# The first expert of a mixture kernel in another order, and every fourth input tile kept on chip

## The reference, cut to what matters

```python
# x: (32, 128, 1024): 4096 tokens of 1024 values
y   = einsum('bct,bcd->bdt', x, w0[cond])            # one 128x128 matrix per batch entry
probs = softmax(y @ gate_w.T)                        # 64 experts
w, sel = top_k(probs, 8);  w = w / sum(w)
# each expert takes its first CAP = 256 tokens, in token order
h   = silu(inp @ wg[e]) * (inp @ wu[e])              # 256 x 384
out = h @ wd[e]                                      # 256 x 1024
x   = x + sum over the experts of w * out, at the token's row
x   = x + second layer (one adapter matrix per batch entry, then a base product
          with a two-of-eight gated low-rank part)
```

## Time and profile before

| | |
|---|---|
| median of three runs | 2400.86 us (2400.47 to 2400.88) |
| the profiled execution | 2414.42 us, span 2412.7 us |
| mean granted clock of PE | 0.994 of full speed |
| PE busy | 2371.8 us (98% of the span) |
| DVE, ACT, POOL busy | 1739.5, 1374.4, 1408.7 us |
| DMA | 582.35 MB, mean 241 GB/s |

### The profile page before, as it was taken

One profiled execution on the slowest core, in us unless ns is written; L12 is line 12 of the kernel. 1 busy time (PEld: TensorE's weight loads), 2 busy tenths in 40 slices (PEclk: granted clock), 3 DMA queues, 4 the chain that ended last, 5 costly groups with the idle time before them and its releaser, 6 DMA issues.

```text
span 2412.7 us, 35618 instructions
## 1 busy us (share of the span) xinstructions
PE 2371.8 (98%) x12877; PEld 2089.1 (87%) x12877; DVE 1739.5 (72%) x2905; ACT 1374.4 (57%) x2288; POOL 1408.7 (58%) x1032
## 2 busy tenths in 40 slices
PE   6998999999999999999999999999999999999999
PEld 4677888888888888888888888888879999999999
DVE  4877888888888887888888888887862255555554
ACT  4766777777677776777777777777751111111110
POOL 4107887777777777777777777777710032222221
PEclk9999999999999999999999999999999999999999
DMA  8988998989999899998989989899875254444441
GB/s 295 366 293 286 292 282 282 279 276 292 286 289 282 277 285 284 280 285 274 283 282 284 281 278 280 278 289 279 276 205 110 76 148 129 129 129 129 129 120 56
DMA packets 249457, 582.35 MB, mean 241 GB/s; under 512 B 82745, under 2 KB 106682, under 8 KB 249154
## 3 DMA queue, kind: packets, MB, share of 16 engines
q1 hardware_dynamic: 182306, 401.18, 50.8%
q0 software_dynamic: 55584, 160.02, 25.6%
q10 hardware_dynamic: 11392, 18.88, 2.1%
HBM read 460.71 MB, written 123.45 MB: 242 GB/s over the span
## 4 chain that ended last, share of the span: by engine, by line
PE 89%; ACT 1%; DVE 1%; DMA 1%; issue 1%; SPq 0%; ACTq 0%; DVEq 0%
PE ps L762 25%; PE ps L775 21%; PE ps L869 16%; PE ps L761 12%; PE ps L827 5%; PE ps L758 4%; PE ps L862 2%; PE ps L759 2%; PE ps L842 1%; PE ps L725 1%; ACT HR L1020 0%; DMA raw<-in_L_ffn_wd 0%; DMA bmR<-accd 0%; DVE LR L1435 0%; DMA x<-in_L_ffn_base_w 0%
## 5 line engine op out<-in xcount | busy, mean ns | idle before, releaser
L762 PE MATMUL ps<-XX,HR 128*128 128x512 f32 x2688 | 958.6, 396 | 0.0
L761 PE MATMUL ps<-XX,LR 128*128 128x256 f32 x2688 | 750.4, 279 | 0.0
L546 POOL DMA_INDIRECT Xg<-yd,idx x504 | 648.0, 1286 | 166.2 <-issue 152.6
L1435 DVE TENSOR_TENSOR LR<-raw,HR 128x1536 fp32r<-128x1536 f32 x384 | 657.3, 1752 | 5.7 <-issue 3.7
L762 PEld LDWEIGHTS ps<-XX,HR 128*128 128x128 f32 x2688 | 505.3, 188 | 103.7
L1020 ACT ACTIVATE HR<-raw 128x1536 fp32r<-128x1536 f32 x384 | 556.4, 1478 | 16.5 <-DMA raw<-in_L_ffn_wd 11.5
L761 PEld LDWEIGHTS ps<-XX,LR 128*128 128x128 f32 x2688 | 507.0, 189 | 17.7 <-issue 0.2
L568 POOL DMA_INDIRECT accd<-ot,toki x128 | 254.2, 1986 | 157.4 <-ACT ot L1074 136.0
L869 PE MATMUL ps<-MH,xT 128*128 128x392 f32 x1536 | 337.2, 345 | 0.0
L775 PE MATMUL ps<-HR,hH 128*128 128x512 f32 x768 | 300.0, 391 | 4.8 <-DVE hL L1479 4.8
L775 PE MATMUL ps<-LR,hH 128*128 128x512 f32 x768 | 303.6, 395 | 0.0
(11 more groups left out here) (203 smaller groups left out, 3344.0 us busy)
## 6 DMA issues: line engine op xcount, KB each, us to landing
raw<-in_L_ffn_wd SPq DMA_DIRECT2D x128, 768.0 KB
raw<-in_L_ffn_wg SPq DMA_DIRECT2D x126, 768.0 KB
raw<-in_L_ffn_wu SPq DMA_DIRECT2D x126, 768.0 KB
xt<-in_x SPq DMA_DIRECT2D x32, 512.0 KB
yd<-yrow ACTq DMA_DIRECT2D x32, 512.0 KB, 6.7
x<-accd SPq DMA_DIRECT2D x32, 512.0 KB, 5.0
out<-osb SPq DMA_DIRECT2D x31, 512.0 KB, 2.9
accd<-xt SPq DMA_DIRECT2D x24, 512.0 KB
```

What stands on the lines that cost most here:

```text
L546: eng.indirect_dma_start(Xg[:, c, q, :], None, yd4, bass.IndirectOffsetOnAxis(ap=idx4[:, e % 4, i:i + 1], axis=0))\
L761: eng.matmul(bank(out, 0, CAP), wl, xx[:, 0:CAP], start=False, stop=False)
L762: mm = eng.matmul(bank(out), wh, xx, start=False, stop=(k == 7))
L1435: eng.tensor_tensor(LR[:, (n + 2) % NHL, :], raw[:, n % NRAW, :], HR[:, (n + 2) % NHL, :].bitcast(F32), ALU.subtract).then_inc(s_L, 1)
```

## The change

Seven things are changed, all of them at the seam of stage 1 and the first expert.

1. `turn_0`: the identity products ahead of `direct_rows` (4) go, and 10 and 44 become 8 and 20.
2. The eight tiles with i % 4 = 3 are not copied from DRAM to DRAM. Seven of them are loaded to places of their own (`xkA`, `xkB`, `xkC`, found by `xin(i)`), which lie in HR and LR buffers that stage 1 doesn't use; the last one stays in `xt[:, 3]`. `store_kept(n)` stores them to `acc` from there: four behind unit 1, four behind unit 5. Semaphores `d_ak[0]` and `d_ak[1]` tell of the two groups.
3. New waits on them: ACT's split of unit 4 on group 0 and of unit 6 on group 1, DVE's split of unit 4 and `turn_x(1, 0)` on group 1, `scatter(0)` on both.
4. SP's units 0 to 3 wait for the row stores of tiles 25 to 28 in place of 28 to 31.
5. DVE: `direct_token(0)` and `direct_token(1)` stand ahead of `tiles(NB - 6)`, and the first waits for all row stores (`d_ys`).
6. ACT, first expert: `uB`, the load of the Silu table, then `high_0`, then `dA`, `dB` and the parts' chain, with shares and `store_w` between the first and the second part, and the unit splits of expert 1 behind the third part except `gA`.
7. DVE, first expert: `uA` ahead of `low_0`; `join(0)` ahead of the last `weigh`/`invert`, which are spread around `product(0)`; `dB`, the turns and sums for expert 1 between the parts; `column(0)`, `column(1)`, `index(2)` behind the third part, then the splits of expert 1.

From the second expert on the order is the same as before.

```diff
-            rest = [i for i in range(NB) if i % 4 >= NS]
-
-            def fill(n):
-                i = rest[n]
-                if n >= 2:
-                    eng.wait_ge(d_ad[n % 2], 16 * (n // 2))
-                eng.dma_start(acc[i * P:(i + 1) * P, :], x_r[i * P:(i + 1) * P, :]).then_inc(d_ad[n % 2], 16)
+            def store_kept(n):
+                i = 4 * n + NS
+                eng.wait_ge(d_x[NS], 16 * (n + 1))
+                eng.dma_start(acc[i * P:(i + 1) * P, :], xin(i)).then_inc(d_ak[n // KEEP], 16)
 
             for n in range(len(units)):
                 if n < NRAW:
-                    i = NB - NRAW + n
+                    i = NB - NRAW - 3 + n
                     eng.wait_ge(d_ys[i % NY], 16 * (i // NY + 1))
...
                 load_unit(n)
-                if n == 7:
-                    for k in range(FILL):
-                        fill(k)
-                if n >= 8 and n - 8 + FILL < len(rest):
-                    fill(n - 8 + FILL)
+                if n == 1:
+                    for k in range(KEEP):
+                        store_kept(k)
+                if n == NRAW + 1:
+                    for k in range(KEEP, NB // 4):
+                        store_kept(k)
...
             def turn_0():
                 eng.wait_ge(s_yr, NB)
-                keep_busy(4)
                 direct_rows()
-                keep_busy(10)
+                keep_busy(8)
                 eng.wait_ge(s_tok, 2)
-                keep_busy(44)
+                keep_busy(20)
...
@@ ACT
+                if n == NRAW:
+                    eng.wait_ge(d_ak[0], 16 * KEEP)
+                if n == 6:
+                    eng.wait_ge(d_ak[1], 16 * KEEP)
...
             split("uA", 0)
+            split("uB", 0)
+            eng.activation(sil[:, 0:1], pf[:, 0:1], ACT.Silu)
             for n in range(4):
                 high_0(n)
-            split("uB", 0)
+            split("dA", 0)
+            split("dB", 0)
+            copy_2(0)
+            silu(0)
+            high_h(0)
             for i in range(NB - 4, NB):
                 share(i)
             store_w(NB - 1)
-            eng.activation(sil[:, 0:1], pf[:, 0:1], ACT.Silu)
-            split("dA", 0)
+            split("gA", 1)
+            copy_2(1)
+            silu(1)
+            high_x(1, 0)
+            high_h(1)
+            high_x(1, 1)
+            copy_2(2)
+            silu(2)
+            spread(2)
+            high_h(2)
+            for k in ("uA", "gB", "uB", "dA"):
+                split(k, 1)
...
@@ DVE
             direct_slots()
-            tiles(NB - 6)
             direct_token(0)
             direct_token(1)
+            tiles(NB - 6)
...
+                if n == NRAW:
+                    eng.wait_ge(d_ak[1], 16 * KEEP)
...
             index(1)
+            split("uA", 0)
             for n in range(4):
                 low_0(n)
-            split("uA", 0)
             split("uB", 0)
             for i in range(NB - 3, NB):
                 tiles(i)
             table_rows()
-            for i in range(NB - 4, NB):
+            split("dA", 0)
+            join(0)
+            for i in range(NB - 4, NB - 2):
                 weigh(i)
                 invert(i)
-            split("dA", 0)
+            product(0)
+            for i in range(NB - 2, NB):
+                weigh(i)
+                invert(i)
+            low_h(0)
+            split("dB", 0)
+            join(1)
+            turn_x(1, 0)
+            product(1)
+            turn_x(1, 1)
+            low_h(1)
+            count(2)
+            token(2)
+            join(2)
+            low_x(1, 0)
+            product(2)
+            low_x(1, 1)
+            low_h(2)
+            column(0)
+            column(1)
+            index(2)
+            for k in ("gA", "uA", "gB", "uB"):
+                split(k, 1)
+            count(3)
+            token(3)
+            split("dA", 1)
```

76 lines of the change are left out of this document (34 added, 42 removed).

## The result

The changed kernel takes 2408.86 us (median of 8 runs, 2407.58 to 2412.56). The kernel before, run beside it, takes 2401.67 us (8 runs, 2400.47 to 2402.71). The ratio is 1.0032, with a 95% interval of 1.0024 to 1.0041: the change costs 7.2 us. The prediction was 2396.5 us with a range of 2391.0 to 2400.6, so it has the wrong sign and misses its range.

A forecast was written before the change was run, and what follows sets the result against it. PE was taken to bound the kernel, at 25.0 us an expert from the third on. PE 4.4 us earlier at the third part of up(2), taken over to the median 2400.86 us, gave 2396.5 us, range 2391.0 to 2400.6.

The forecast's parts named there:

- What bounds the kernel: Whole kernel: PE, busy 2371.8 of 2412.7 us; only its idle or low-clock time in the first experts can be won.
- The sum: PE at the third part of up(2): 254.9 - 250.5 = 4.4 us earlier, then 25.0 us an expert as before.
- Its eight issues took 11.3 us: POOL's gather_x(2): starts at 204.5 instead of 207.39, keeps its 11.3 us, last issue out at 215.8.
- The start: First expert: direct_token(0) near 165.0, 1.4 us earlier; high_0 at 175.3, 5.4 us earlier; up(0) at 178.5 instead of 183.92.
- The new wait: DVE's split of dA in expert 0 waits about 6 us for the kept stores, the last landing near 188.
- the stores are hidden: Rival on the kept stores: they land before about 184, 6.5 to 10 us won, 2392 us; chance 0.24.
- DVE's walk: DVE's queue in the first expert, walked from 188.1: index(2) done at 204.5, before at 205.27.
- From the last issue to `join(3)`: Behind gather_x(2): 3 us to land and turn, then low_x and join; from 215.8 to join(3) at 222.9.
- The clock: Third part of up(1): PE idles 4.2 us, restarts at half clock and loses 2.0 us.
- The gap at `up(0)`: PE idle 2.8 us between transposes and up(0): at most 2.0 us of low clock, covered, so nothing in the sum.
- POOL behind `gather_x(2)`: POOL's 1.62 us idle ahead of scatter(0) goes; last gather for expert 3 and join(6) come 4.5 us earlier.
- slower by over 0.2%: Rival: direct_token(0) waits for all 32 row stores, landing d after 165.0; over 0.2% slower from d = 9.2 us; chance 0.10.

The follow-up runs named there:

- experiment 15: Kernel before with fewer identity products, join(2) moved first, and gather_x(e + 2) ahead of scatter(e - 1) on POOL for every expert: 2465.51 us, ratio 1.0269.
- experiment 5: The changed kernel again, no edit, for a second profile: 2421.12 us, ratio 1.0026 to the kernel before.
- experiment 1: The kernel before again, no edit, for a second profile: 2413.83 us, ratio 0.9997.
- experiment 6: Changed kernel with count(3) and token(3) between the second and third of DVE's four splits behind index(2): 2420.38 us, ratio 1.0020 to the kernel before.
- experiment 13: Changed kernel with index(2) behind DVE's four splits instead of ahead of them: 2408.36 us, ratio 1.0028 to the kernel before.
- experiment 3: Changed kernel with the second group of four kept stores issued behind unit 3 instead of unit 5: 2419.05 us, ratio 1.0023 to the kernel before.
- experiment 7: Changed kernel with count(2), token(2), spread(2) and index(2) moved earlier: 2415.27 us, ratio 1.0001 to the kernel before.
- experiment 8: Changed kernel with 14 identity products added behind the transposes, ahead of up(0): 2420.04 us, ratio 1.0023 to the kernel before.
- experiment 9: Changed kernel with raw weight loads waiting for row stores 28 to 31, as in the kernel before: 2420.76 us, ratio 1.0029 to the kernel before.
- experiment 4: Kernel before with only the kept tiles, their stores and waits, in its own queue orders: 2414.27 us, ratio 1.0000.
- experiment 16: Kernel before with kept tiles and 28 identity products, but old queue orders, no early SP start, no row-store wait: 2402.46 us, ratio 1.0002.
- experiment 10: Kernel before with the changed kernel's turn_0 and ACT and DVE orders, but old fills, SP queue and buffers, no row-store wait: 2418.57 us, ratio 1.0010.
- experiment 2: Kernel before with only fewer identity products, none ahead of direct_rows, then 8 and 20: 2409.38 us, ratio 0.9984.

## Why the prediction was wrong

**What bounds the kernel** was read rightly: PE, and only its idle and slow stretches in the first experts. From the third part of `up(2)` to the end of the span every profile but one has 2154.7 to 2159.5 us, whatever its kernel; the one is experiment 15 (2205.2), which makes the scatter late. The place of the loss was foretold too: PE idles before the third part of `up(1)` and restarts at half clock. Its size was not.

**The sum, redone.** The prediction had PE at the third part of `up(2)` at 250.6; experiment 5, with stage 1 as long as in the profile before, has 261.63. That is 6.7 us later than before (254.93) and 7.9 later than in experiment 1 (253.76), so a loss of the measured size (6.5 us beside experiment 5, 7.2 in the first comparison) already stands at this product; what single executions differ by behind it allows no finer account. The forecast is missed by 11.0 us: 3.1 at the start of `up(0)` (181.59, predicted 178.5), 7.3 from there to the third part of `up(1)` (52.4, predicted 45.1), and 0.6 from there on (27.6, predicted 27.0).

**The largest step that failed: "Its eight issues took 11.3 us", taken over to a place where they take 16.5.** The prediction moved `gather_x(2)` to the start of DVE's four splits and kept its old length. The first issue takes 7.2 us there, 3.9 before two splits, and 0.95 behind them (experiments 5, 6, 13); only in experiment 3 it takes 2.2 before four. That is 5.2 of the 11.0 us, and 5.2 of the 5.6 us by which `join(3)` comes later behind `up(0)` in the first profile than predicted (50.0, 44.4). This step alone doesn't decide the sign. With 2.21 us for the first issue in the profile of experiment 3, or 3.88 in that of experiment 6, the kernels are no better by the ratios (1.0023 and 1.0020, beside 1.0026), and the rows are turned later behind their issue. Only the earlier index, which takes the gather out of the run's start and puts it ahead, wins 5.9 us (experiment 7), and that just makes up the loss. The steps below are needed for the rest. The Trainium skill has a mechanism near this one (SBUF — State Buffer, section "SBUF: two separate sides"): a DMA issued from GpSimd's queue has its descriptors written by GpSimd, and VectorE can lock it out of the ports they share while it runs an operation in a two-port mode. For operations with two inputs in SBUF, as the splits are, it names contention only against a GpSimd operation that reads SBUF; the issue has its indices in SBUF (`idx`), so it may be one. I had not weighed that rule. The traces show the issue waiting for a split (0.95 us without, 2.24 under one); why one issue waits for four of them no run here shows.

**The start.** `direct_token(0)` was to be 1.4 us earlier, at 165.0. In six profiles of the changed kernel and its variants (experiments 3 and 5 to 9; the kernel before has 165.66 beside them) it lies between 165.44 and 168.60, never earlier by more than 0.2 us and mostly later: what PE saved in front of it, something in the last tiles took back. The early weights (change 4) are the likeliest. Where stage 1 is long, every profile with them has `Gj` at 166.57 or later; without them it is at 165.66 or earlier but for 166.42 in the earlier trace rows and 167.41 in experiment 4, both with the old order and all identity products. Where it is short, those with them have 154.26 or later, those without 153.76 or earlier. Experiment 9, which takes back change 4 alone, has 165.44. These are single executions, 1 to 3 us apart, so it isn't proven; and the prediction had said only that the row stores "may land later", at no price. In experiment 5 this is the whole of the miss at the start: `Gj` 3.6 us late, `Gj` to `up(0)` 13.0 us, predicted 13.5. In the first profile there is a second one: `high_0` was to start 10.3 us behind `Gj` and has 12.75, behind a wait of 2.18 us for `uB`'s weights, where experiment 5 has 9.8 and no wait. The prediction took all four units as landed.

**The new wait** was sized well and judged too important. DVE waits 7.47 us for the stores, predicted about 6. Without it (experiment 3) `index(2)` comes only 2.8 us sooner behind `up(0)` (24.2, 27.0). The rival "the stores are hidden" is refuted by the wait itself, and experiment 3 shows that it would not have helped: even with the wait gone the kernel is slower than before.

**DVE's walk** gave `index(2)` 26.0 us behind `up(0)`; it is 27.0, and 28.3 in experiment 5. That is 5.7 us (27.0) behind its old distance, and the prediction saw this, but set it against a start 5.4 us earlier, which came 0.5 to 2.3 us earlier (181.59 in experiment 5; 183.92 before and 182.05 in experiment 1). So the gather was no longer ahead of its old time even before its first issue was held.

**From the last issue to `join(3)`** 7.1 us were predicted, 6.0 measured: right for a gather as late as this one. Where the issues are out sooner it takes 9.0 to 9.9 us (experiments 3, 6 and 7), so a correct, shorter gather would have made this term too small.

**The clock.** 2.0 us were counted for a wait of 4.2 us at `up(1)`; the wait is 8.4 us and costs 2.3 (5.2 us for the first sixteen products of the third part, 2.9 at full clock). The gap at `up(0)` was put at nothing in the sum, and experiment 8 agrees: 1.1 us or less, within the scatter.

**POOL behind `gather_x(2)`.** The idle time before the scatter is gone as predicted: it starts 6.4 us behind the last gather's start, where before it was 8.9. But the whole chain begins 9.2 us later behind `up(0)` (43.0, 33.8). PE doesn't wait for `join(6)` all the same, since it has lost its time at `join(3)` already.

**The parts by whole kernels.** Fewer identity products have -0.0016, kept tiles +0.0018 once the filler is short, the rest +0.0030 (changed kernel against experiment 16) or +0.0026 (experiment 10 against 2, the order alone). With the first figure the sum, +0.0032, is the measured ratio by construction, since each kernel is compared with the next; and that "rest" holds change 4 and the wait for the row stores beside the order. With the second it is +0.0028, measured 1.0032 and 1.0026: that agreement is a finding. So the order is what takes the gain back, and costs about 6 us. The prediction put slower by over 0.2% at 0.10, for another reason, `direct_token(0)` waiting for all row stores; that is not the cause: `Gj` is released by PE in both profiles.

## What to carry to other kernels

Before a POOL gather is moved, look at what DVE does in the 10 us behind the new place: a run of large DVE operations without a break can hold the issue that starts at its head for as long as the run lasts (six of seven profiles here), so the index should be ready before the run, not at its start. And an edit that costs nothing alone may cost something beside another: a filler that looks like waste can be the cover of a late load, and when it is cut, the next thing to look at is every DMA that used to land under it. Where the profiled execution lies far above the median, first find the stretch in which it does.
